# Graph attention, gather stage: transposes placed between the row products on TensorE, and the maximum placed behind the fourth sum on VectorE

## What is computed

```python
h = features @ W_layer.T + b_layer
a1 = (h @ w_a1.T + b_a1)[:, 0]
a2 = (h @ w_a2.T + b_a2)[:, 0]
v = jax.nn.leaky_relu(a1[row] + a2[col], negative_slope=0.01)
m = jax.ops.segment_max(v, row, num_segments=n)
ev = jnp.exp(v - m[row])
s = jax.ops.segment_sum(ev, row, num_segments=n)
att = ev / s[row]
out = jax.ops.segment_sum(att[:, None] * h[col], row, num_segments=n)
```

## Time and profile before

| | us |
|---|---|
| median of three runs | 2673.71 (2671.26 to 2674.08) |
| the profiled execution's own time | 2673.89 |
| its span | 2672.2 |
| gather stage, from the first gather to DVE's last sum | about 355 to 1712 |
| mean granted TensorE clock over the span | 0.884 |

### The profile page before, as it was taken

How to read it: one execution, slowest core, us unless ns; L and a number is a source line. 1 busy time by engine, 2 the same in 40 slices (tenths; PEclk the granted TensorE clock), 3 DMA queues, 4 the chain that set the end, 5 groups by cost and what they waited for, 6 DMA issues and landing times.

```text
span 2672.2 us, 44967 instructions
## 1 busy us (share of the span) xinstructions
PE 2246.7 (84%) x12642; PEld 1845.2 (69%) x12659; DVE 1756.8 (66%) x5731; ACT 1261.8 (47%) x3795; POOL 1289.9 (48%) x1320
## 2 busy tenths in 40 slices
PE   3789848887788888888777788869999999999997
PEld 1566626665566666665555566667999999999997
DVE  8677747777777777777777776777555555555553
ACT  7666645555555555555555555651222222222221
POOL 0000045666666666666666666007444444444443
PEclk8899958788988888788999987659999999999999
DMA  2243333443444344443444435590222222222221
GB/s 80 91 137 120 123 87 93 111 108 109 114 112 111 106 112 114 112 109 110 112 114 112 108 106 86 109 326 16 35 37 33 36 35 35 37 35 35 37 35 27
DMA packets 141978, 237.84 MB, mean 89 GB/s; under 512 B 29546, under 2 KB 101066, under 8 KB 140970
## 3 DMA queue, kind: packets, MB, share of 16 engines
q0 software_dynamic: 65664, 143.64, 24.4%
q1 hardware_dynamic: 76074, 91.34, 10.4%
HBM read 182.34 MB, written 52.53 MB: 88 GB/s over the span
## 4 chain that ended last, share of the span: by engine, by line
PE 49%; DVE 23%; issue 13%; another core or an unknown queue 5%; DVEq 4%; ACT 3%; DMA 2%; POOL 0%; SPq 0%; ACTq 0%; POOLq 0%
PE psum L1695 19%; PE psum L1728 10%; DVE arena L1291 9%; PE psum L1195 7%; DVEq L1310 3%; PE psum L524 3%; PE psum L1203 2%; PE psum L1187 1%; DVE arena L1302 1%; DVE arena L1361 1%; DVE arena L1333 1%; PE psum L503 1%; DVE arena L1355 1%; DMA arena<-mix_inputs 1%
## 5 line engine op out<-in xcount | busy, mean ns | idle before, releaser
L1149 POOL DMA_INDIRECT arena<-table,arena x878 | 854.4, 973 | 483.0 <-issue 250.9
L1195 PE MATMUL psum<-arena 128*128 128x257 f32 x1756 | 652.0, 492 | 254.5 <-DVE arena L1291 156.3
L1195 PEld LDWEIGHTS psum<-arena 128*128 128x128 f32 x1756 | 338.6, 228 | 469.5 <-issue 372.9
L1291 DVE SCALAR_TENSOR_TENSOR arena<-arena,psum 128x257 f32 x878 | 420.5, 479 | 308.2 <-remote 181.1
L1695 PE MATMUL psum<-arena 128*128 128x128 f32 x4620 | 550.8, 275 | 0.6 <-ACT arena L1750 0.6
L1695 PEld LDWEIGHTS psum<-arena 128*128 128x128 f32 x4620 | 541.4, 192 | 6.7 <-issue 0.9
L1825 POOL DMA_INDIRECT out<-arena x105 | 170.6, 1625 | 382.1 <-ACT arena L1757 379.1
L1222 ACT ACTIVATE arena<-arena 128x128 f32<-128x128 bf16 x880 | 280.9, 390 | 119.3 <-DVE arena L1305 69.8
L1728 PE MATMUL psum<-arena 128*128 x1260 | 290.7, 379 | 0.8 <-ACT arena L1757 0.8
L1235 ACT ACTIVATE arena<-arena 128x128 f32<-128x128 bf16 x880 | 281.2, 391 | 7.1
L1187 PEld LDWEIGHTS psum<-arena 128*128 128x128 f32 x1760 | 244.2, 209 | 23.8 <-issue 18.0
(11 more groups left out here) (344 smaller groups left out, 3127.1 us busy)
## 6 DMA issues: line engine op xcount, KB each, us to landing
mix_inputs<-arena SPq DMA_DIRECT2D x147, 128.0 KB, 2.2
arena<-table,arena POOLq DMA_INDIRECT x878
arena<-in_x SPq DMA_DIRECT2D x98, 128.0 KB, 2.9
arena<-mix_inputs SPq DMA_DIRECT2D x49, 256.0 KB
arena<-in_w SPq DMA_DIRECT2D x6, 1364.0 KB, 6.5
out<-arena SPq DMA_DIRECT2D x50, 128.0 KB, 3.2
table<-arena SPq DMA_DIRECT2D x49, 129.0 KB, 2.2
arena<-mix_inputs SPq DMA_DIRECT2D x49, 128.0 KB, 3.2
```

What stands on the lines that cost most here:

```text
L1149: pool.indirect_dma_start(rows_in[j][:, q * TW:(q + 1) * TW], None, table_d[:, :], bass.IndirectOffsetOnAxis(ap=col_all[:, t:t + 1], axis=0))\
L1195: last = mm(psum[4 + q][:, 0:C + 1], weight[b][:, q * P:(q + 1) * P], rows_in[g][:, q * TW:q * TW + C + 1], start=True, stop=True)
L1291: v.scalar_tensor_tensor(here, here, alpha[(j - 5) % RING][:, q:q + 1], psum[4 + q][:, 0:C + 1], ALU.mult, ALU.add).then_inc(S("acc_done"), 1)
```

## The change

It does two things, in the gather stage alone.

On PE, the transposes of step i, which stood as a block behind the four row products, are placed one by one behind each row product: row product 0, transpose 0, row product 1, transpose 1, and so on. The wait for `member_ready` at i - 1, which stood before the transposes, now stands before the first row product. The count of quarters in the last step is written in another way (`t * G + q < USED`) and comes out the same.

On DVE, the third score operation (which gives `z_ready`) and the third and fourth sums are placed ahead of the maximum.

```diff
-                if live(i, 4):
-                    b, g, t = j % 2, (j - 4) % RING, i - 4
-                    for q in range(REST if t == NG - 1 else G):
+                if live(i, 0) and due(i - 1):
+                    pe.wait_ge(S("member_ready"), i - 1)
+                b, g, t = j % 2, (j - 4) % RING, i - 4
+                for q in range(G):
+                    if live(i, 4) and t * G + q < USED:
                         pe.wait_ge(S("weight_ready"), t * G + q + 1)
                         if due((t - 1) * G + q + 1):
                             pe.wait_ge(S("acc_done"), (t - 1) * G + q + 1)
                         last = mm(psum[4 + q][:, 0:C + 1], weight[b][:, q * P:(q + 1) * P], rows_in[g][:, q * TW:q * TW + C + 1],
                                   start=True, stop=True)
-                if live(i, 0):
-                    b = j % 2
-                    if due(i - 1):
-                        pe.wait_ge(S("member_ready"), i - 1)
-                    for q in range(G):
+                    if live(i, 0):
                         pe.wait_ge(S("masked_ready"), i * G + q + 1)
                         last = nc.tensor.transpose(psum[b][:, q * P:(q + 1) * P], masked[b][:, q * P:(q + 1) * P], ident[:, :])
                 last.then_inc(S("pe_step"), 1)
@@
                 add(i, j, 1, columns)
                 exponents(i, j, 1)
+                exponents(i, j, 2)
+                add(i, j, 2, columns)
+                add(i, j, 3, columns)
                 if live(i, 1):
                     if due(t):
                         dve.wait_ge(S("nb_steps"), t)
                     v.tensor_reduce(tile_max[:, :], psum[b].rearrange("p (q r) -> p q r", q=G)[:, :, :], AX.X, ALU.max)\
                         .then_inc(S("max_done"), 1)
-                exponents(i, j, 2)
-                add(i, j, 2, columns)
                 if live(i, 1):
@@
                     v.tensor_tensor(mix_b[m % MS], psum[3][:, C:2 * C], mix_b[m % MS], ALU.add).then_inc(S("half_ready"), 1)
-                add(i, j, 3, columns)
                 if live(i, 1):
                     dve.wait_ge(S("lin_steps"), t + 1)
```

## The result

| | before | after |
|---|---|---|
| median of nine runs, us | 2673.93 (2671.26 to 2674.65) | 2680.54 (2678.41 to 2686.15) |
| span of the profiled execution, us | 2672.2 | 2678.8 |

The ratio is 1.0028, with an interval from 1.0018 to 1.0038. The forecast was 2672 and "the same". The time lies in the range given (2658 to 2682), on its slower side, but it is a loss that can be told from no change, and none was forecast.

What follows compares the result with a forecast made beforehand. The gather stage was taken as paced by its gathers, eight per 12.0 us pair of steps. 0 for 104 pairs and -2 us at the end, against 2673.89, gave 2671.9, so 2672 us; range 2658 to 2682.

Steps and rivals of the forecast that it cites:

- The pace of the pairs: Gather stage: eight gathers take 12.0 us per pair of steps at any clock, so 0 gain for 104 pairs.
- rival A: Gather stage: late semaphore is an effect, not the pace; the shorter loop saves 166 us, 2507 us; chance 0.05.
- What DVE loses: DVE's step: operations now waiting for something just issued cost 0.3 us a step, bounds 0 and 0.4.
- DVE's pair is 10 to 10.8 us, below 12.0: DVE in the gather stage: two steps without waiting, the added 0.3 us each included, fit into the gathers' pace.
- Rival C: DVE's scan and `lin` meet late semaphores late in a pair: 49 pairs, 37 us slower, 2709 us; chance 0.12.
- POOL's pauses: POOL's gathers: mid-run pauses of up to 1.04 us go, worth 0.0 to 0.13 us a pair, taken as 0.
- Behind the last tick: Steps after the gathers run out: last wait gains 1.4 us, the steps behind some 0.6, together -2 us.
- PE's half: PE's loop: transposes between products, with earlier sums, shorten DVE's first sum to `pe_step` by 1.4 us, 4.6 to 3.2.
- The estimate of 10.6 us for eight gathers: Gathers: 1.3 us each for 132 KB, by which a pair could be 1.4 us shorter, the kernel some 145 us faster.
- What would show it: Signs in the new trace: "remote" some 89 times, over 181 us; POOL's mid-run pauses gone; ticks 12.0 us apart within 0.05.

Runs made afterwards that it cites:

- z_half: Kernel before with 129 of 258 columns per gathered row from the ninth step on, on a chip with 12.0 us pairs: 2673.70 us, ratio 1.0004.
- e1_pe_only: Kernel before with only PE's new order of transposes, DVE's order old: 2463.45 us, ratio 1.0004.
- h_pe_only: Kernel before with only PE's new order of transposes, run once more on another set: 2461.36 us, ratio 0.9994.
- c_before: Kernel before, unchanged, traced on a chip where no semaphore is held: 2464.93 us, ratio 0.9994.
- z_three: Changed kernel with the maximum behind the third sum and sum 3 behind lin again, on a chip with 12.0 us pairs: 2673.71 us, ratio 1.0003.

## Why the prediction was wrong

The sum was 0 for the 104 pairs and -2 us behind the last tick. It measured +4.65 and +2.4; the rest, up to the first tick and behind the stage, is -0.4. Both terms fail at the same place, what DVE loses, and the first one fails at one more, the comparison with 12.0 us.

**The pace of the pairs** was right for this chip. 93 of 104 pairs keep 12.0 us at every clock, and `z_half` shows that the bytes don't set it. It was not asked from where the pace comes, and on most chips it isn't there. On those, what rival A takes for granted is so, but its price has the other sign. It took DVE's step at 5.2 us in place of 6.0; it is 5.05 before, set by POOL's issue, and 5.53 after, set by DVE.

**What DVE loses** is the term that was sized wrong. It read "The nearest row is the 0.14 us between sum 0's end and sum 1", "bounds are 0 and 3 x 0.14 = 0.4 us a step. I take 0.3". It measured 0.63 us, above the upper bound. The 0.14 us are the gap between two rows, and that is not what such a wait costs. A sum starts 0.62 us behind the sum that it waits for, whether two small operations stand between (sum 0 and sum 1) or none (sum 2 and sum 3, now). What doesn't wait starts 0.40 us behind a sum, so a bare wait costs 0.22. And three other pairs at 0.11 to 0.12 us each were added. The rows that would have told it were in the trace of before: the tail at 1355, 1361 and 1366 is a chain with nothing between, and its starts are 0.19 to 0.20 us apart (1688.93 and the two rows behind it, above) where others are 0.07.

**"DVE's pair is 10 to 10.8 us, below 12.0"** is the comparison that failed: the forecast took for granted that what fits into the pace costs nothing. By its steps DVE's pair is 10.6 us without mixing and up to 11.4 with it, still below 12.0. But the late semaphores come on top, and the sum left them out. Rival C had them: in the late part of a pair a dependent operation waits for a late semaphore. C's place and mechanism are what happened, and its price and its count were off. It expected scan and `lin` to be hit in 49 pairs, for 37 us. What was hit were the two last operations of the tail, in 35 pair ends for 22 before. In twenty of them that made the first sum over 1 us late, and in eleven, together with the lower clock, PE's first step passed 6.0 us. The price was 4.65 us. "Against it: a DVE that lags moves PE's first `pe_step` back, and POOL's pause returns" was used as an argument against a loss, and it is how the loss comes about: a pause that is long enough ends the run later.

**POOL's pauses** were taken to go, at 0. The fifth gather of a pair follows the fourth without a pause (after the bare 0.30 us) in 63 of 104 pairs, where it was 43. But in the eleven long pairs the idle before it is 1.19 to 1.75 us, where before it was nowhere over 1.12. The price read from one pair (0 to 0.13 us) was of idle below 1.05 us, where the pair still lasts 12.0.

**Behind the last tick** the forecast had -2 us and it was +2.4. "DVE bounds most of them, so the gain is the last wait" was sound, but then DVE's 0.6 us a step had to be put against it: 1.4 us over six steps. The other 0.9 us are one step at a lower clock.

**PE's half** did what was said and is worth nothing where it was run alone: `e1_pe_only` 1.0004 and `h_pe_only` 0.9994, on chips where POOL's issue sets the pace. By the Trainium skill, Perfetto Trace Analysis, section Optimization Strategy, one finds the gaps of the engine that one works for and makes the dependencies that end them start sooner. In the changed kernel the idle before PE's row products fell from 254.5 to 217.9 us, but not the time. The estimate of 10.6 us for eight gathers from the skill's DMA: Bandwidth & Descriptors, section Measured, is near the 10.1 us a pair of `c_before` by chance. A gather's row packets take 0.80 us in the trace and not the estimate's 1.3, and the 10.1 us are POOL's issues.

**What would show it** asked for "remote" ahead of DVE's first sum "still some 89 times, but with more than 181 us". It is 51 times with 65.6 us: DVE comes later to the tick, not earlier. The bound on the ticks' distance, 0.05 us, was kept (0.045), and it was too wide: over 104 pairs it lets 5.2 us through, as much as a measurement can tell. That the time still lies in the range is luck: the range was made wide for C at a quarter of its price, and what came was C's mechanism at an eighth of it, with a second loss at the end.

## What to carry to other kernels

An operation that stands between two dependent ones on the same engine is not in the way, it is cover: before moving it, price each pair that becomes adjacent from a pair that is adjacent already. A pace that comes from elsewhere hides a longer step only until its latest member passes the point at which the pace reacts (here PE's first step at about 6.0 us of 12.0), so look at the latest case and not at the mean, and at what a lower granted clock adds in the same place. And a change that costs little where a slow pace hides it can cost much where the pace is faster: 0.3% and 3.7% here.

## What was unexpected of the hardware

- The same kernel takes 2462 to 2466 us on five chips, and 2657 to 2674 on two others and in the first runs. On the former a step takes 5.05 us and no wait of DVE or POOL in the stage is put down to "remote", on the latter 6.00 (no trace of the kernel before was taken on the one with 2657). The gathers' transfers take the same time on both, and the traces of the slower kind hold about half as many semaphore updates. The cause isn't shown.
- Where semaphores come late in a pair, they come at set places. The last operation of DVE's tail, where it waited for more than 0.25 us, started 3.1, 2.3, 1.6, 0.9 or 0.2 us ahead of the tick and not between, in `before`, `after` and `z_three`: some 0.7 us from one place to the next.
- Where a pair takes 12.0 us, halving the bytes and the row packets of each gather leaves it at 12.005. The number of gathers and of their rows stayed as it was; whether one of them sets the 12.0 us was not tried.
- On DVE, an operation of 128 x 4 that waits for the one just ahead starts 0.12 us later than one that doesn't, and a sum of 128 x 257 that waits for another just ahead 0.22 us later.
- A copy of 0.20 us on POOL between two gathers added 0.09 us, and one of 0.33 us (160 columns) 0.21: the 0.30 us between two issues can be used.
